# Three tiles of a mixer-and-experts kernel are placed by the caller, and a one-column tile moves behind `knee`

## What is computed

```python
def mixer(x):                                   # on layernorm(x)
    x = silu(depthwise_conv(lin(x, w1), conv_w, conv_b))
    A_bar = exp(-softplus(lin(x, dl_w, dl_b)) * lin(x, A_w, A_b))
    h = cumsum(lin(x, B_w, B_b) * cumprod(A_bar, axis=1), axis=1)
    y = lin(h, C_w, C_b) + lin(x, D_w, D_b)
    return y + lin(y * silu(lin(y, w2)), w3)

def ffn(x):                                     # on layernorm(x)
    xn = layernorm(x) * gamma + beta
    comb = the two largest of softmax(xn @ router), made to sum to 1
    return sum(comb[:, e] * swiglu(xn, e) for e in range(8)) + swiglu(xn, shared)

x = x + layernorm(mixer(layernorm(x)))
x = x + layernorm(ffn(layernorm(x)))
```

## The kernel before

| tile | bytes | starts | mod 64 | mod 256 |
|---|---|---|---|---|
| `ident` | 512 | 23584 | 32 | 32 |
| `w_both` | 36864 | 24128 | 0 | 64 |
| `w_full` | 6208 | 60992 | 0 | 64 |
| `ones` | 2048 | 67200 | 0 | 128 |
| `x_in` | 8192 | 69248 | 0 | 128 |
| `u` | 8208 | 77440 | 0 | 128 |
| `cv` | 8192 | 85664 | 32 | 160 |
| `linear` | 4 | 93856 | 32 | 160 |
| `xs_hi`, `xs_lo` | 8192 each | 93888, 102080 | 0 | 192 |
| `delta`, `decay`, `a_cum`, `bx`, `h` | 4096 or 2048 | 110272 to 122560 | 0 | 192 |
| `h_hi`, `h_lo` (two each) | 8192 each | 126720 to 151296 | 0 | 0 |
| `s`, `g`, `xr` | 4096 each | 159488 to 167680 | 0 | 0 |
| `xnt`, `w_sh`, `n2` | 20480, 6144, 8320 | 171776, 192256, 198400 | 0 | 0 |
| `cdb`, `knee` | 8, 16 | 206720, 206752 | 0, 32 | 128, 160 |
| `st` | 192 | 206784 | 0 | 192 |

## Time and profile before

### The profile page before, as it was taken

The page is one execution under the profiler, slowest core; times in us unless marked ns, Lnnn a source line. Parts: engine busy times, 40 slices in busy tenths (PEclk is TensorE's granted clock), DMA queues, the critical chain, the costliest instruction groups (busy, mean ns, idle before and its releaser), DMA issues.

```text
span 1187.3 us, 23315 instructions
## 1 busy us (share of the span) xinstructions
PE 1096.2 (92%) x7492; PEld 973.6 (82%) x7492; DVE 833.9 (70%) x2113; ACT 654.8 (55%) x1325; POOL 302.9 (26%) x358
## 2 busy tenths in 40 slices
PE   3989999899979989999999999999999999999940
PEld 2765776677757656999999999999999999999940
DVE  5986899898888667666666666666666666666645
ACT  6768867778584354444444444445444444444425
POOL 1142033723441624121221122122112211221225
PEclk9999999999999999999999999999999999999975
DMA  8654766973665779532231245555922356211239
GB/s 304 220 194 173 248 231 211 316 237 142 221 232 168 249 260 344 158 67 58 54 71 18 36 130 194 189 172 184 370 34 36 85 199 230 36 28 25 36 87 214
DMA packets 96617, 191.70 MB, mean 161 GB/s; under 512 B 8768, under 2 KB 59456, under 8 KB 96576
## 3 DMA queue, kind: packets, MB, share of 16 engines
q1 hardware_dynamic: 80160, 170.38, 41.9%
q0 software_dynamic: 16416, 20.85, 10.2%
HBM read 295.62 MB, written 86.41 MB: 322 GB/s over the span
## 4 chain that ended last, share of the span: by engine, by line
PE 80%; DVE 7%; issue 3%; DMA 3%; ACT 2%; POOL 2%; SPq 1%; another core or an unknown queue 0%; DVEq 0%; ACTq 0%; POOLq 0%
PE bank L1336 12%; PE bank L1335 12%; PE bank L1337 12%; PE bank L462 11%; PE bank L1346 6%; PE bank L1348 6%; PE bank L1347 6%; PE bank L456 4%; PE bank L458 4%; PE bank L457 4%; PE bank L1323 1%; DVE xr L1476 1%; POOL xs_scratch L1142 1%; DVE a_cum L867 1%; SPq L441 1%
## 5 line engine op out<-in xcount | busy, mean ns | idle before, releaser
L1335 PE MATMUL bank<-h_hi,w_both 128*128 128x256 f32 x936 | 268.2, 287 | 0.2 <-DVE cv L1452 0.2
L1445 DVE TENSOR_SCALAR cv<-bank 128x256 f32<-128x256 f32 x312 | 132.3, 424 | 193.1 <-PE bank L1337 193.1
L1285 POOL DMA_INDIRECT acc_scratch<-cv,ids x78 | 126.1, 1616 | 554.3 <-DVE cv L1424 513.6
L1337 PE MATMUL bank<-h_hi,w_both 128*128 128x256 f32 x936 | 261.2, 279 | 0.0
L1336 PE MATMUL bank<-h_hi,w_both 128*128 128x256 f32 x936 | 261.2, 279 | 0.0
L1395 ACT ACTIVATE cv<-cv 128x256 f32<-128x256 f32 x312 | 130.3, 418 | 233.8 <-DVE cv L1445 233.0
L1387 ACT ACTIVATE h_hi<-cv 128x256 fp32r<-128x256 f32 x312 | 129.8, 416 | 115.0 <-DVE cv L1452 115.0
L1335 PEld LDWEIGHTS bank<-h_hi,w_both 128*128 128x128 f32 x936 | 177.4, 190 | 0.4 <-issue 0.4
L1336 PEld LDWEIGHTS bank<-h_hi,w_both 128*128 128x128 f32 x936 | 176.1, 188 | 0.0
L1337 PEld LDWEIGHTS bank<-h_hi,w_both 128*128 128x128 f32 x936 | 175.7, 188 | 0.0
L1452 DVE TENSOR_TENSOR cv<-bank,cv 128x256 f32<-128x256 f32 x312 | 132.6, 425 | 47.4 <-ACT cv L1395 34.6
(11 more groups left out here) (227 smaller groups left out, 2391.5 us busy)
## 6 DMA issues: line engine op xcount, KB each, us to landing
w_both<-w_split SPq DMA_DIRECT2D x228, 768.0 KB
xs_hi<-w_split SPq DMA_DIRECT2D x38, 768.0 KB
xs_lo<-w_split SPq DMA_DIRECT2D x38, 768.0 KB
e_raw<-w_e SPq DMA_DIRECT2D x64, 384.0 KB
w_split<-e_high SPq DMA_DIRECT2D x64, 384.0 KB
w_split<-e_raw SPq DMA_DIRECT2D x64, 384.0 KB
u<-xs_scratch SPq DMA_DIRECT2D x40, 260.0 KB
x_in<-x SPq DMA_DIRECT2D x8, 512.0 KB
```

Of the source, the lines that this page charges most:

```text
L1335: nc.tensor.matmul(out, e_hi[f][:, cols], xg_hi[:, par, c, :], start=c == 0, stop=False)
L1337: i = nc.tensor.matmul(out, e_lo[f][:, cols], xg_hi[:, par, c, :], start=False, stop=c == DC - 1)
L1445: nc.vector.tensor_scalar(gate[:, f % 4, :], gu_ps[f % 2][:, 0:G], CLIP, -CLIP, ALU.min, ALU.max).then_inc(clipped, 1)
```

## The change

`w_both`, `w_full` and `ones` are made in `program`, in a scope of their own around the call of `mixer`, and handed over as arguments. They come behind `neg_half` and ahead of `x_in`, as before. Inside `mixer`, `linear` is made after `knee` and no longer between `cv` and `xs_hi`. The line that names the two halves of `w_both` moves up. No instruction, wait, loop or queue is edited.

```diff
@@ def mixer
-        w_both = sb("w_both", [P, 2 * W_COLS], F32R)
-        w_full = sb("w_full", [P, F_COLS])
-        ones = sb("ones", [P, HALF])
+        w_hi, w_lo = w_both[:, 0:W_COLS], w_both[:, W_COLS:2 * W_COLS]
         x_in = sb("x_in", [P, LT, D])
         u = sb("u", [P, DC, L + 2])
         cv = sb("cv", [P, DC, L])
-        linear = sb("linear", [P, 1])
         xs_hi = sb("xs_hi", [P, DC, L], F32R)
...
         knee = sb("knee", [P, HC])
+        linear = sb("linear", [P, 1])
         st = sb("st", [P, LT, 6])
...
-        w_hi, w_lo = w_both[:, 0:W_COLS], w_both[:, W_COLS:2 * W_COLS]
@@ def program
-        mixer(nc, ...)
+        with ExitStack() as first:
+            def sb1(name, shape, dt=F32):
+                return first.enter_context(nc.sbuf_tensor(name, shape, dt))
+
+            w_both = sb1("w_both", [P, 2 * W_COLS], F32R)
+            w_full = sb1("w_full", [P, F_COLS])
+            ones = sb1("ones", [P, HALF])
+            mixer(nc, ..., w_both, w_full, ..., ones, ...)
```

More of the change, by code:

```diff
@@ L57, with mixer @@
 XS = 5
-def mixer(nc, x, w_e, w_s, weights, full, consts, shared, xs_dram, x1_dram, acc_dram, fill, vec, ident,
-          tok_id, pad, zeros, neg_half, tables, group_expert, group_change, group_row, group_code, out):
+def mixer(nc, x, w_e, w_s, weights, full, consts, shared, xs_dram, x1_dram, acc_dram, fill, w_both, w_full, vec, ident,
+          tok_id, pad, zeros, ones, neg_half, tables, group_expert, group_change, group_row, group_code, out):
     with ExitStack() as ctx:
@@ L1531, in program @@
         neg_half = sb("neg_half", [P, LT])
[L1532 to L1538, removed]
+        with ExitStack() as first:
[4 more added lines that the diff above has]
+            ones = sb1("ones", [P, HALF])
+            mixer(nc, d["x"], d["w_e"], w_s,
+                  [(DL_AT, d["dl_w_t"], DC), (A_AT, d["A_w_t"], DC), (B_AT, d["B_w_t"], DC), (C_AT, d["C_w_t"], HC),
+                   (DD_AT, d["D_w_t"], DC)],
+                  [(W1_AT, d["w1_t"], DC), (W2_AT, d["w2_t"], DC), (W3_AT, d["w3_t"], DC), (RT_AT, d["router"], DC)],
+                  d["vecs"], [(SGU_AT, d["sgu"], DC), (SDN_AT, d["sdn"], SC)], xs_dram, x1_dram, acc_dram,
+                  fill, w_both, w_full, vec, ident, tok_id, pad, zeros, ones, neg_half, tables,
+                  group_expert, group_change, group_row, group_code, out)
 def kernel(**inputs):
```

## The result

The changed kernel is slower: 1200.55 us in the median of 13 executions (1196.29 to 1205.66) against 1192.41 us (1187.01 to 1198.65) for the kernel before in the same sessions. The ratio is 1.0079, with a 95% interval of 1.0058 to 1.0099. The prediction said no effect, 1196.5 us, in a range of 1187 to 1204. The absolute time lies in it, but the forecast of no movement fails: 8 us are lost, and the interval leaves no room for nothing.

The account below looks back on a forecast made before the run. TensorE's matmul stream was taken to bound the kernel, strictly from 480 to 1142 us. All terms were 0: 1189.42 + 0 = 1189.4 us for the profiled execution, 1196.5 for the median, range 1187.1 to about 1204.

Parts of the forecast that it names:

- no effect: Whole kernel: the change does nothing on the chip, median stays 1196.5 us; chance 91%.
- GpSimd rival: GpSimd's wide subtraction, line 1125, doubles on shifted tiles; about 12 us lost, 1208.5; chance 2%.
- transfer rival: Loads into shifted tiles are slow: two on the chain, 7.02 and 3.88 us, doubled; 10.9 us, median 1207.4; chance 2%.
- the 5.5 to 5.9 that the prediction allowed: Sign at the kernel's last store, from `s`: it lands in 5.5 to 5.9 us.
- The 1.2 us more: Last store from `s` at rest 224: 39 beats in place of 32, at most 1.2 us on 5.5; median 1197.7.
- the TensorE term: Matmuls streaming from shifted tiles: w1 and w2 products both have a 592 ns median, so cost taken as 0.
- upper bound of 3.7 us: All matmuls: by the minima 2 ns or 0.3% slower, over 1096.2 us of TensorE work.
- Nothing can be gained: Shifted tiles: no row shows a tile at rest 32 faster than its fellow at rest 0.
- rival of 64-byte lines: TensorE fetches 64-byte lines: 7.3 ns more on each of 5076 shifted streams, 37 us, median 1233.6; chance 3%.
- the signs that the prediction named: Equal counts, line 1335 at 279 to 287 ns, second part 99.6% busy, line 1125 1.3 to 1.5 us, w2 592 ns.
- within 1%: Whole kernel: measured time within about 12 us of before, covering forecast, load rival and half the GpSimd one; 94%.

Follow-up runs that it names:

- e1: Kernel before with only `linear` moved behind `knee`, the three tiles still made in `mixer`: 1192.42 us against 1185.07, ratio 1.0064.
- e2: Kernel before with `carry_h` moved behind `knee`, so `h_hi` and all behind it go down 32 bytes, ring slots 6 and 7 stay: 1196.29 us against 1185.07.
- e5: Kernel before with `linear` made ahead of `w_both`: `w_both` to `cv` go up 32 bytes, `xs_hi` to `n2` stay: 1190.84 us against 1179.73.
- m1: TensorE alone, computation left out: groups of 24 matmuls of 256 columns, weights moved 32 bytes per group, up and down: 24 took 2.72 or 2.88 us.
- e4: Kernel before with a 32-byte spacer ahead of `w_both`, moving every tile from there on up by 32 bytes: 1181.98 us against 1185.07.
- e7: Kernel before with a 256-byte spacer ahead of `carry_a`, moving `h_hi` and all behind it up: 1195.30 us in one execution.
- e8: Kernel before with a 64-byte spacer ahead of `carry_a`, putting `h_hi` at distance 0 to `w_both`: 1204.05 us against 1194.13.
- e9: Kernel before with a 128-byte spacer ahead of `carry_a`: gate_up goes from distance 64 to 192, down from 192 to 64: 1202.27 us in one execution.
- e3: Kernel before with `linear` made between `h` and `carry_a`: `xs_hi` to `h` go down 32 bytes, `h_hi` and all behind stay: 1182.26 us against 1185.07.
- e10: Kernel before with spacers and `h_hi[1]` moved: all ring slots at distance 64 to `h_hi[0]`, `h_hi[1]` at rest 64: 1184.19 us against 1185.58, ratio 0.9978.
- e6: Kernel before with 128 bytes ahead of `xs_hi` and 128 more ahead of `carry_a`, so slots 6 and 7 stand to `h_hi` like the others: ratio 0.9987.

## Why the prediction was wrong

**What held.** The three tiles and the two names cost nothing that shows (e1). The counts are equal. The tile placement was read rightly as the only thing that reaches the chip, and the stretch from 480 to 1142 us as the one that nothing covers. The range holds the measured time in part by luck: the kernel before came out at 1192.41 us here, 4.1 under the 1196.53 that the prediction laid its result on, and 1196.53 with the 8.1 us of the loss would be 1204.7, outside. In-place ScalarE work on `delta` at rest 32 takes 624 ns (623 before), VectorE's subtraction 416 as before, GpSimd's line 1125 (now 1122) has a median of 1296 ns (1302), so the GpSimd rival is dead. The w2 product from `s` at rest 32 has a median of 592, as before. The transfer rival didn't come: the two on the chain that the prediction names are, against the earlier trace rows,

```profile
1.85 6.23 DMA xnt<-dl_w_t
...
1160.42 4.08 DMA xnt<-acc_scratch
```

10.3 us together, and 10.9 before. The prediction overlooked a third load into a shifted tile on the chain of before:

```profile
222.78 3.86 DMA xr<-x
```

It isn't on the chain of the changed kernel, and its median from issue to landing is 4.9 us before and 4.6 in e1. The last store from `s`, by the view of DMA issues,

```profile
out<-s SPq DMA_DIRECT2D x1, 512.0 KB, 6.3
```

landed after 6.3 us (5.5 before), outside the 5.5 to 5.9 that the prediction allowed. It isn't the placement: in e1 and e2, with `s` at rest 224 as in the changed kernel, the same store landed after 5.5 and 5.4 us, and in e5, with `s` at rest 0, after 6.7. The 1.2 us more that the prediction estimated for such a store doesn't show in e1 and e2 either.

**The step that failed** is the TensorE term: "By the medians the price is 0", taken from the w1 product with `cv` at rest 32 against the w2 product with `s` at rest 0. It measured 0.44 us a pass, 8.6 us in all. Three faults lie in it.

- The ruler was another form. Those are 512 columns in 592 ns, one every 429 ns by their starts, far longer than the 190 ns that each of their weight loads takes; the second part has a matmul every 113 to 120 ns and a load, 188 to 190 ns long, always under way. The slack is the likely reason why they show nothing; no run varies it by itself. The 512-column matmuls of the earlier trace rows, with steps of 232 ns, do show an effect of 1 ns (below).
- It was an alignment of one tile that was tested, where the effect is of two. Both sides of the comparison differed in the rest of the moving operand, and the weights were left out. With `w_full` at rest 64 by 256 the distances were 160 for `cv` and 64 for `s`, by chance the slowest and the fastest of m1, and the steps were 429 ns in both.
- The upper bound of 3.7 us was worked out from the same wrong form and was no bound: the loss is 0.44 us in each of 19.5 passes, 8.6 us (7.6 from the first to the last matmul with slot 6, where the kernel before had 1 us more of idle time). "Nothing can be gained" was wrong by the same ruler: slot 7 went from 118 to 113 ns. The rival of 64-byte lines had the right place, a full-speed stream that no row of before covered, got a price of 37 us where some 8 were due, and 3% of the chance. Its mechanism is refuted by e4 and e5. Of the signs that the prediction named, the durations in slot 6 (279 ns) and the busy share (319.52 of 320 us) stayed inside their bounds; the pace, which shows the loss with 118.1 ns (320/2709) where 117 stood, was watched only for the 124 of the line rival.

There was a warning in the trace. 320/2735 is 117 ns, where the starts of the same trace hold runs of 113. The 287 ns in the earlier trace rows beside the 279 in the earlier trace rows are none: they are a mean that 79 of the 936 matmuls, those behind a turn of rows with 355 ns and more, lift. Two paces of one instruction with no wait between them mean that something besides the instruction sets the time, and the addresses were the one thing that the change altered.

**The range and the chances.** 94% for "within 1%" is met by 0.79%, and the median of 1200.55 lies under 1204, but as forecast "no effect" is wrong. The change costs two thirds of a per cent in e1 and 0.8% in the larger comparison, and with 13 executions on each side that can be told from nothing.

**What stays open.** Why the pace repeats with 256 bytes, and what decides between 113 and 118 ns at distances 64 and 192, was not shown; no run looks inside. Also open is the spread of 9 us between executions of one kernel: the first matmul of slot 6 came at 481.4 us in the changed kernel, 474.9 in e1 and 472.4 in e5, which have equal passes, so the spread arises in the first part. What the change costs there is below that spread, but the steps show it: the mean step of the 512-column matmuls that stream from `xs_hi` and `xs_lo` against `w_both`, taken over the steps below 250 ns, is 232.3 to 232.5 ns in the six traces that keep their distance of 128 (before, e2, e4, e7, e8, e9) and 233.5 in the four that have 160 (after, e1, e3, e5). For 672 of them that is 0.8 us.

## What to carry to other kernels

In this stream of matmuls, which leaves TensorE no idle time, the place of a tile is a parameter like any other: the step depends on the distance by 256 bytes between the weights and the moving operand, from 113 to 120 ns here for 256 columns, and a tile made or removed ahead of one of them changes it. Which distance is good has to be measured for each form: with 512 columns 0 is the fastest (see below), with 256 it is among the slowest. So count matmuls in a full stretch, not their durations, and compare steps from start to start; and before an edit of declarations is called free, see that the operands of the hot loop keep their distances. The loop can be tried on TensorE alone: it gave the kernel's pass to 14 ns for three placements, and was 0.1 us too fast for that of e10.

## What the runs showed of the hardware that was not expected

- One and the same matmul, 128 rows by 256 columns with its weights loaded anew each time, steps at 113.6 to 120.1 ns in the mean of a group depending on the two addresses and on what ran before, at granted clock 1.00 (2.4 GHz) and with no other engine at work (m1). The Trainium skill, SBUF — State Buffer, Who interferes with whom, counts two SBUF read ports for TensorE, one for the moving operand and one for the weight load, and calls them independent; "PE and ACT never wait on anyone." As far as other engines go the trace agrees (34.49 us a pass alone and in the kernel). Between TensorE's own two reads the trace speaks against independence: one sequence takes 34.28 to 35.39 us a pass by how the two addresses stand to each other.
- The period is 256 bytes: a move by 256 left 2833 matmuls in the stretch against 2834 (e7), a move by 64 left 2775 (e8).
- At distance 64 the pace depends on what ran before: 117.9 ns behind a group at distance 32, 113.6 behind one at 96, which itself ran at 118.8.
- The order of the distances is another for 512 columns. The streams from `xs_hi` and `xs_lo` against `w_both` step at 229.2 and 229.5 ns at distance 0 (e6, e10), 232.3 at 128 (before) and 233.5 at 160 (after); those from `h_hi` and `h_lo` at 228.4 at distance 0 (e8) and 232.9 at 64 (before).
- A start 32 bytes off a multiple of 64 costs this stream nothing as such (e4, x2839).
